# All source-order places scanned in the head stage, none in the first attention stage

## What is computed

```python
xn = _layernorm(x)
x = x + _L0_gnn_ref(xn, src, dst, Wq, bq, Wk, bk) + _L0_mix_ref(xn, ...)   # edge softmax; linear attention + MLP
x = x + _L0_ffn_ref(_layernorm(x), ...)                                    # MLP on the 3124 best rows
xn = _layernorm(x)
x = x + _L1_gnn_ref(xn, edge_weight, W, b, src, dst) + _L1_mix_ref(xn, ...)
x = x + _L1_ffn_ref(_layernorm(x), ...)
```

```python
support = jnp.matmul(x, W)
gathered = support[dst] * edge_weight[:, None]
out = segment_sum(gathered, src, n) + b
```

## Time and profile before

| what | us |
|---|---|
| median of 2 runs (7586.34 to 7595.01) | 7590.68 |
| the profiled execution | 7602.24 |
| its span | 7600.5 |
| head, from the span's start to ln_a's first load | about 190 |
| sums0, first to the next stage's first DMA | 431 |
| ln_b | 62 |

### The profile page before, as it was taken

The page is one execution under the profiler, slowest core; times in us unless marked ns, Lnnn a source line. Parts: engine busy times, 40 slices in busy tenths (PEclk is TensorE's granted clock), DMA queues, the critical chain, the costliest instruction groups (busy, mean ns, idle before and its releaser), DMA issues. The chain is left out here.

```text
span 7600.5 us, 120043 instructions
## 1 busy us (share of the span) xinstructions
PE 4920.3 (65%) x21606; PEld 3536.8 (47%) x21607; DVE 3625.5 (48%) x12097; ACT 2115.7 (28%) x4904; POOL 4936.4 (65%) x5789
## 2 busy tenths in 40 slices
PE   0663436889999999719926639265656565655692
PEld 0333323555666666507813528244444444434582
DVE  8882545666667777731122330633333333333314
ACT  6321333445555555404423213000000000001450
POOL 0387377777777777567747667577777777772002
PEclk9886767999999999959968969678787878788896
DMA  3101003444444444300010000033333333331000
GB/s 85 38 2 11 6 4 89 116 116 116 116 116 116 116 116 116 81 3 15 3 38 4 4 12 3 14 106 105 106 105 105 106 106 105 106 105 41 13 0 35
DMA packets 504121, 493.93 MB, mean 65 GB/s; under 512 B 373899, under 2 KB 401027, under 8 KB 503299
## 3 DMA queue, kind: packets, MB, share of 16 engines
q0 software_dynamic: 200192, 432.72, 20.7%
q1 hardware_dynamic: 177155, 55.21, 3.4%
q10 hardware_dynamic: 126720, 5.46, 1.1%
HBM read 462.74 MB, written 30.23 MB: 65 GB/s over the span
## 5 line engine op out<-in xcount | busy, mean ns | idle before, releaser
L1060 POOL DMA_INDIRECT XN<-table,XN x3128 | 2988.8, 955 | 832.0 <-issue 704.5
L487 POOL DMA_INDIRECT records<-slot_rec,slot_pos x1564 | 1604.0, 1026 | 466.2 <-issue 466.2
L1374 PE MATMUL gcn_psE<-XN,gcn_pE 128*125 x3520 | 1187.7, 500 | 929.7 <-SPq L1040 914.6
L1374 PEld LDWEIGHTS gcn_psE<-XN,gcn_pE 128*125 128x125 f32 x3520 | 832.1, 246 | 1285.0 <-issue 1127.1
L1194 PE MATMUL gat_psE<-XN,gat_pE 128*125 x3520 | 876.0, 392 | 3.4 <-ACT gat_pE L1247 2.9
L1402 DVE TENSOR_TENSOR room<-room,gcn_psE 125x256 f32 x440 | 185.3, 421 | 1195.8 <-PE gcn_psE L1374 1194.5
L1194 PEld LDWEIGHTS gat_psE<-XN,gat_pE 128*125 128x125 f32 x3520 | 635.4, 191 | 84.4 <-issue 4.6
L73 POOL TENSOR_TENSOR cell<-cell 1x1 int32<-1x1 int32 x874 | 174.6, 200 | 657.8 <-DMA slot_pos<-spill_pos 613.9
L602 ACT ACTIVATE gcn_w_stage<-room 125x512 f32 (+1 forms) x25 | 15.6, 622 | 2082.5 <-PEq L115 2082.5
L539 POOL TENSOR_TENSOR X<-X,room x150 | 120.6, 836 | 620.8 <-DVE room L581 620.8
L1390 DVE TENSOR_SCALAR gcn_pE<-iota_n,gcn_lk,gcn_rec 128x125 f32<-128x125 f32 x1760 | 504.8, 359 | 16.0
(11 more groups left out here) (399 smaller groups left out, 7712.7 us busy)
## 6 DMA issues: line engine op xcount, KB each, us to landing
XN<-table,XN POOLq DMA_INDIRECT x3128, 2.8
records<-slot_rec,slot_pos POOLq DMA_INDIRECT x1564
XN<-records SPq DMA_DIRECT2D x782, 6.0 KB, 1.7
table<-XN SPq DMA_DIRECT2D x10, 1250.0 KB
gat_rec<-records ACTq DMA_DIRECT2D x440, 6.0 KB
gcn_rec<-records ACTq DMA_DIRECT2D x440, 6.0 KB
out_x<-X SPq DMA_DIRECT2D x5, 1250.0 KB
X<-in_x SPq DMA_DIRECT2D x1, 5600.0 KB
```

Source lines behind the costliest of these rows:

```text
L487: pool.indirect_dma_start(out=rec_d[self.which], out_offset=bass.IndirectOffsetOnAxis(ap=slot_pos[:, h, j:j + 1], axis=0), in_=slot_rec[:, ...
L1060: pool.indirect_dma_start(out=rows_t[:, s, j, :], out_offset=None, in_=table, in_offset=bass.IndirectOffsetOnAxis(ap=rec_g[:, s, j, 1:2].b ...
L1374: last = pe.matmul(psE[d][0:B, 0:D], pE[:, d, j, :], rows_t[:, slot_of(g), j, :].rearrange("p a w -> p (a w)"), start=(j == 0), stop=(j == ...
```

## The change

`HEAD_COLS` becomes `EC`, so the head scans all 1564 columns, and its store (line 289) carries all of `posi`. sums0 loses its 51 scans over 1258 columns, the store at line 817 with its wait, and two semaphores. One turn of the mover goes from sums0 to ln_b: sums0 5, att0 3, ln_b 1.

```diff
-HEAD_COLS = 306
+HEAD_COLS = EC
@@ attention_sums
-                pos_own, pos_done = sem(name + "_pos_own"), sem(name + "_positions")
...
                         if edge:
-                            sp.wait_ge(pos_done, 1)
-                            sp.dma_start(spill_pos[1][:, HEAD_COLS:EC], posi[:, HEAD_COLS:EC]).then_inc(stored, 16)
                             sp.wait_ge(qk_done, 3 * NC)
                             sp.dma_start(rows(table)[:, :, D:D + SMALL], q_all[:, :, :]).then_inc(stored, 16)
-                        sp.wait_ge(stored, 16 * (7 if edge else 5))
+                        sp.wait_ge(stored, 16 * (6 if edge else 5))
...
-                        places = Places(dve, Steps(dve, pos_own), blkf, base, pos, posi, HEAD_COLS, EC - HEAD_COLS)
-                        with loop(dve, NC, places.st, 10 if edge else 0) as k:
+                        with loop(dve, NC) as k:
...
-                            if edge:
-                                places.blocks(k * 2, 2)
...
-                        if edge:
-                            places.finish(pos_done)
@@ the stages
-                kvd = attention_sums(c1, "sums0", A["L0_mix_Wkv"], edge, table0, turns=6)
+                kvd = attention_sums(c1, "sums0", A["L0_mix_Wkv"], edge, table0, turns=5)
...
-            layer_norm("ln_b", U, U, affine=(A["L0_mix_ln1_g"], A["L0_mix_ln1_b"]), turns=0)
+            layer_norm("ln_b", U, U, affine=(A["L0_mix_ln1_g"], A["L0_mix_ln1_b"]), turns=1)
```

## The result

The changed kernel takes 7689.5 us (two runs: 7674.5 and 7704.4) against 7590.7 before. The ratio is 1.0126, with a 95% interval of 1.0075 to 1.0177: slower, by less than 2%. The profiled execution took 7704.4 us, and all rows of "after" come from it.

What follows compares the result with a forecast made beforehand. It took DVE to bound the head and POOL's mover, slowed by DVE's scans, to end sums0. +223 - 136 + 0 = +87 us on the profiled 7602.2 gave 7689, or 7677 for the median; range 7658 to 7710.

Steps and rivals of the forecast that it cites:

- Head, +223: Head: 1258 more columns cost 4.364 us a block over 51 blocks, with DVE alone on the path; +223 us.
- The slope: Head: cost per column between widths 306 and 1258, together 3.469 ns for scan, copy and mask, carried on to 1564.
- sums0, -136: sums0: POOL still ends it, with 10 half turns at 21.59 us in place of 12; 517.5 instead of 653.7, -136 us.
- the 11.5 that I kept: sums0: 11.5 us between POOL's last instruction and the next stage's first DMA, taken as unchanged.
- The split: sums0: of the 136 us gained, 43 from two half turns less and 93 from the quicker pace without scans.
- The rival of the attention or q's store: sums0: attention or q's store finishes last, stage end 528 in place of 517.5, total 7688; chance 0.14.
- The slow mover: sums0: half turns stay at 32.3 us without scans, only 29 us come back, total 7785; chance 0.05.
- the cheap wide scans: Head: wide scans cost 2.7 us a block in place of 4.36, so no slowdown, total 7591; chance 0.02.
- The lines on the Trainium skill: sums0: by the page's port rules scans could not hold up the mover, giving 7785; by the trace rows 7677.
- ln_b, 0: ln_b: the added turn ends at 878.9, hidden under DVE's work until 888.5; 0 us.
- My bound of +7: ln_b: upper bound on the added turn's cost, two half turns at the slow 32.3 us reaching 896.
- The sum: Whole kernel: +223 head, -136 sums0 and 0 ln_b give +87 us, 1.1% more.

Runs made afterwards that it cites:

- add_copy: The changed kernel with two predicated copies of 128x1258, results unused, added to each chunk of sums0; on chip A sums0 took 304.8 us, a half turn 23.1.
- add_mask: The changed kernel with two is_equal masks of 128x1258, results unused, added to each chunk of sums0; on chip A sums0 took 296.2 us, a half turn 22.0.

## Why the prediction was right, step by step

*Head, +223.* Measured +221.3. The slope held outside its two widths, for the scan best: 3461 ns (predicted 3.46 us), 1886 for the copy (1.91), 626 for the mask (0.63). The store of the places left at 383.10 (384).

*sums0, -136.* Measured -139.0. POOL's first instruction came 67.1 us into the stage (67.5), its ten half turns took 511.0 to 727.3 = 216.3 (215.9), and the tail behind it was 8.6 us in place of the 11.5 that I kept: that is the difference. The split was slightly off: I gave 43 to the moved turn and 93 to the quicker half turns; measured one after the other, the turn first, they are 48 (2.8 of it the shorter tail) and 90.

*The rival of the attention or q's store.* It was not near. Chunks took 9.26 us, not 10, and the granted clock was 1.00 (2.4 GHz) while PE was busy for 149.9 of 168 us, against 0.85 with 192 of 267 before; the q store left at 686.4 and its transfer was over by about 708, 19 us ahead of POOL. I had charged the chunks too much, from the one chunk that the trace of before showed without scans. It was the first, which is no measure of the others: in the changed kernel too the first took 11.3 us.

*The slow mover and the cheap wide scans.* Both fell: 21.55 us a half turn, and 4.34 us a block more in the head (221.3 / 51). The experiments with added work show why the first was wrong: POOL waits for wide scans, copies and masks, the scans above all, and they had left sums0; DVE's remaining work, or a reduction, does not hold it. The lines on the Trainium skill in the prediction set 7785 beside the page's inference; the measured 7689.5 goes with the rows.

*ln_b, 0.* Measured +0.2 on chip A, in all five profiles that have the turn there. (My bound of +7 was reckoned too low: two half turns at 32.3 us would have ended at 878.9 + 2 x 10.7 = 900, 11 us late. Nothing hung on it.) Its busy row, with POOL's 36 instructions beside DVE's 157:

```profile
910.00:972.10 62.10, 0.00 (x0) 0.00 (x0) 58.59 (x157) 1.61 (x2) 36.55 (x36) 0.50 0.04 6
```

*The sum.* Predicted +87, measured +82.7 in the touched stages. The forecast of 7677 lies 12.5 us under the measured 7689.5, which is inside the range. The touched stages would have given 7590.7 + 83 = 7673; in the profiled execution the missing part is in stages that I set to 0, att1 above all. Its rows (length, busy times, granted clock) are, before:

```profile
4157.80:4305.00 147.20, 95.26 (x500) 79.41 (x500) 68.31 (x225) 40.55 (x75) 99.24 (x108) 0.89 0.04 4
```

after, in the profile of the result:

```profile
4233.80:4408.10 174.30, 122.16 (x500) 100.35 (x500) 68.30 (x225) 40.53 (x75) 98.96 (x108) 0.75 0.03 4
```

in the repetition of the changed kernel:

```profile
4242.30:4396.10 153.80, 102.00 (x500) 84.31 (x500) 68.36 (x225) 40.52 (x76) 98.89 (x108) 0.86 0.04 4
```

and with only the turn moved:

```profile
4102.30:4246.40 144.10, 86.70 (x500) 73.92 (x500) 68.34 (x225) 40.62 (x76) 98.92 (x108) 0.93 0.04 4
```

The instruction counts and the busy time of DVE, ACT and POOL are equal; only PE's busy time goes with the granted clock. So the 27 us go with PE's clock, in a stage where PE is the busiest engine, and not with more work. The four later runs on chip A leave less unexplained: 90.9 us measured, 84 in the touched stages. Whether the change causes the lower clock is open. Four profiles on chip A with the scans in the head (the two above, add_copy 157.1, add_mask 158.7) have 154 to 174 us, two with the scans in sums0 144 and 147; that leans towards a cause, but no step from the scans to this stage, over 3000 us later, was found, and neither of the outcomes that I had written down came.

## What to carry over

Before work is moved out of a loop that it fills, ask what else runs beside it there and how that is slowed by it. Here the scans, which add 221 us in the head, had cost only 90 us in the old place: they lay beside a mover that ends the stage, and cost what they slowed it. What the mover lost there hung on how long the single DVE instruction was that it had to wait out, and of which kind, not on how busy DVE was. The part of the move that pays may be separable: one turn of the mover, put under a layer norm that leaves POOL idle, gave 0.5% by itself and needed no scan to move. Sum by the last finisher of each stage, and leave some 10 us for the clock in stages that nobody touched.

## What I had not expected of the hardware

- This kernel took 7600 us on one chip and 10011 us on two others. On those, in sums0, ACT began 71 us and DVE 30 us after the matmuls that they wait for were over, while POOL issued an indirect DMA every 1.26 us; DVE scans that hold POOL back took the stalls away (sums0 351.6 against 461.2), reductions did not (461.5). The head, ln_g and the last feed-forward stage take the same on both.
- An indirect DMA that begins under a `tensor_tensor_scan`, a `copy_predicated` or an `is_equal` mask of 128x1258 ends 0.76 to 0.83 us after that instruction's end, in place of 0.96 us after its own start. For the scan (2.8 us long) that is mostly 2.4 us, for the copy (1.55 us) 1.1 to 1.4, for the mask (0.53 us) up to 1.3. Under a `tensor_reduce` of 2.9 us it stays 0.96.
- The scan is linear in columns from 306 to 1564: 842, 2821 and 3461 ns. Predicated copy (495, 1567, 1886) and mask (300, 551, 626) nearly so.
- The same attention stage, with the same instructions, took between 144.1 and 174.3 us on one kind of chip, with a granted clock of 0.93 to 0.75.
